# Moving a bias from TensorE to GpSimd in a relational layer, and giving VectorE's small steps two inputs

## The reference

```python
def _layernorm(x, axis=-1, eps=1e-05):
    m = jnp.mean(x, axis=axis, keepdims=True)
    v = jnp.var(x, axis=axis, keepdims=True)
    return (x - m) / jnp.sqrt(v + eps)

def _L0_gnn_ref(x, adj, relation, weight, bias):
    rel_ids = jnp.arange(1, weight.shape[0] + 1, dtype=relation.dtype)
    masks = (relation[None] == rel_ids[:, None, None, None]).astype(x.dtype)
    h = jnp.einsum('rbnm,bmd->rbnd', masks, x)
    y = jnp.einsum('rbnd,rdo->bno', h, weight)
    return y + bias

x = _layernorm(x + _L0_gnn_ref(x, L0_gnn_adj, adj, L0_gnn_weight, L0_gnn_bias), axis=-1)
```

## Time and profile before

| | us |
|---|---|
| median of 3 runs | 119.49 |
| lowest and highest | 118.33, 120.13 |
| the profiled execution | 118.53 |
| its span in the trace | 116.7 |
| busy TensorE, VectorE, ScalarE, GpSimd | 102.6, 95.0, 84.6, 75.7 |

### The profile page before, as it was taken

One profiled execution on the slowest core, in us unless ns is written; L12 is line 12 of the kernel. 1 busy time (PEld: TensorE's weight loads), 2 busy tenths in 40 slices (PEclk: granted clock), 3 DMA queues, 4 the chain that ended last, 5 costly groups with the idle time before them and its releaser, 6 DMA issues.

```text
span 116.7 us, 1943 instructions
## 1 busy us (share of the span) xinstructions
PE 102.6 (88%) x587; PEld 85.5 (73%) x587; DVE 95.0 (81%) x242; ACT 84.6 (72%) x114; POOL 75.7 (65%) x78
## 2 busy tenths in 40 slices
PE   5966379994999999999999999999999999999800
PEld 2333378683889888888898889898888888889600
DVE  0089967633989899999999999999999999996960
ACT  0433199179868997899999999999999889974410
POOL 6069038000095998599759898999899759953640
PEclk9999999999999999999999999999999999999996
DMA  3999999999999999999999999999999997030441
GB/s 87 396 433 429 415 438 427 415 432 418 418 424 424 424 424 417 417 424 424 414 431 421 414 428 413 429 413 427 421 427 418 404 420 314 10 142 38 171 152 53
DMA packets 7362, 42.16 MB, mean 361 GB/s; under 512 B 819, under 2 KB 1206, under 8 KB 3254
## 3 DMA queue, kind: packets, MB, share of 16 engines
q1 hardware_dynamic: 7200, 41.95, 86.9%
q10 hardware_dynamic: 150, 0.07, 0.2%
HBM read 37.82 MB, written 4.19 MB: 360 GB/s over the span
## 4 chain that ended last, share of the span: by engine, by line
PE 48%; DMA 21%; DVE 15%; POOL 8%; issue 3%; ACTq 1%; POOLq 0%; DVEq 0%
PE h_ps L187 32%; DMA adj_sb<-in_adj_dram 17%; PE y_ps L199 8%; PE tp_ps L178 7%; DMA bias_rows<-in_L_gnn_bias_dram 4%; DVE bias_parts L491 4%; POOL scale L217 4%; DVE mask L429 3%; DVE stats L205 3%; POOL x_lo L170 2%; DVE total L443 2%; PE y_ps L194 2%; DVE var_eps L214 2%; DVE mean_var L210 1%; ACTq L379 1%
## 5 line engine op out<-in xcount | busy, mean ns | idle before, releaser
L350 ACT ACTIVATE maskT<-tp_ps 128x2048 fp32r<-128x2048 fp8e5 x32 | 60.2, 1881 | 14.9 <-PE tp_ps L178 14.8
L429 DVE TENSOR_SCALAR mask<-adj_sb 128x2048 uint8<-128x2048 uint32 x32 | 39.5, 1267 | 12.4 <-DMA adj_sb<-in_adj_dram 12.4
L217 POOL TENSOR_TENSOR scale<-var_eps,power 128x4 f32<-128x4 f32 (+1 forms) x17 | 36.3, 2137 | 0.9 <-DVE var_eps L214 0.7
L187 PE MATMUL h_ps<-maskT,x_hi 128*128 128x512 f32 (+1 forms) x144 | 34.2, 379 | 2.6 <-ACT maskT L350 2.5
L187 PE MATMUL h_ps<-maskT,x_lo 128*128 128x512 f32 (+1 forms) x144 | 34.3, 380 | 0.4 <-POOL x_lo L170 0.4
L187 PEld LDWEIGHTS h_ps<-maskT,x_hi 128*128 128x128 f32 x144 | 24.3, 189 | 7.7 <-ACT maskT L350 3.9
L187 PEld LDWEIGHTS h_ps<-maskT,x_lo 128*128 128x128 f32 x144 | 24.1, 189 | 4.5 <-POOL x_lo L170 0.7
L178 PEld LDWEIGHTS tp_ps<-identity,mask 128*128 128x128 f32 x128 | 19.8, 202 | 6.4 <-DVE mask L429 2.7
L178 PE MATMUL tp_ps<-identity,mask 128*128 128x128 f32 x128 | 20.2, 281 | 3.4 <-DVE mask L429 3.4
L170 POOL TENSOR_TENSOR x_lo<-x_sb,x_top 128x1024 fp32r<-128x1024 f32 x8 | 19.2, 2402 | 0.0
L307 POOL TENSOR_SCALAR minus_mean<-mean_var 128x4 f32<-128x4 f32 (+1 forms) x16 | 4.0, 248 | 22.5 <-DVE var_eps L214 21.6
(11 more groups left out here) (30 smaller groups left out, 40.4 us busy)
## 6 DMA issues: line engine op xcount, KB each, us to landing
adj_sb<-in_adj_dram SPq DMA_DIRECT2D x32, 1024.0 KB, 18.0
x_sb<-in_x_dram SPq DMA_DIRECT2D x8, 512.0 KB, 12.1
out_dram<-out_sb SPq DMA_DIRECT2D x7, 512.0 KB, 18.5
out_dram<-out_sb SPq DMA_DIRECT2D x1, 256.0 KB, 2.3
out_dram<-out_sb SPq DMA_DIRECT2D x2, 128.0 KB, 2.6
w_sb<-in_L_gnn_weight_dram ACTq DMA_DIRECT2D x1, 64.0 KB, 7.1
bias_rows<-in_L_gnn_bias_dram ACTq DMA_DIRECT2D x3, 0.5 KB
```

What stands on the lines that cost most here:

```text
L187: last = nc.tensor.matmul(h_ps[:, bank, 0:n], (x_hi, x_lo)[part][:, slot, t, :], maskT[:, places, t // WORD, t % WORD, :], start=(first an ...
L217: nc.gpsimd.tensor_tensor(scale[:, slot, tiles], var_eps[:, slot, tiles], power[:, tiles], ALU.pow).then_inc(done, by)
L350: nc.scalar.activation(maskT[:, u % NMT], turned_codes(u % NTP), ACT.Copy, accum_out=counts[:, u:u + 1]).then_inc(expanded, 1)
L429: nc.vector.tensor_scalar(mask[:, u % NMASK], adj_sb[:, u % NADJ].bitcast(u32), CAP, SET, ALU.min, ALU.mult).then_inc(masked, 1)
```

## The change

The bias no longer goes through TensorE. One transfer spreads it over all partitions, and GpSimd adds it to x in place, once per batch, after the last mask of that batch. VectorE's add waits for that (`biased`). The bf16 parts, their splitting and placing are gone. The variance plus epsilon and the normalising on VectorE take a form with two tensor inputs: epsilon comes from a small tile, and the scale is repeated over 128 columns as the second input. GpSimd takes the scales once for a whole batch, for batches 0 to 5; the last two go in halves and quarters as before. Normalising comes one half later on VectorE and on ScalarE. x_lo of batch 0 is made by VectorE, and GpSimd makes x_lo before x_hi of the following batches. TensorE's projection of half 1 comes one turn earlier.

```diff
-        def spread_bias(y, tiles):
-            n = tiles.stop - tiles.start
-            nc.tensor.matmul(y[:, 0:n, :], spread[:, :], bias_parts[:, 0:n, :], start=True, stop=False)
+        def add_bias(x_slot, done):
+            nc.gpsimd.tensor_tensor(x_sb[:, x_slot], x_sb[:, x_slot],
+                                    bias_rows[:, :].unsqueeze(1).to_broadcast([P, TILES, D]), ALU.add).then_inc(done, 1)
...
-            nc.vector.tensor_scalar(var_eps[:, slot, tiles], mean_var[:, slot, tiles, 1], EPS, None, ALU.add).then_inc(done, by)
+            n = tiles.stop - tiles.start
+            nc.vector.tensor_tensor(var_eps[:, slot, tiles], mean_var[:, slot, tiles, 1], eps[:, 0:n], ALU.add).then_inc(done, by)
...
-                last = nc.vector.tensor_scalar(out_sb[:, b, s, :], total[:, place, s, :], mean_var[:, slot, s, 0:1],
-                                               scale[:, slot, s:s + 1], ALU.subtract, ALU.mult)
+                last = nc.vector.scalar_tensor_tensor(out_sb[:, b, s, :], total[:, place, s, :], mean_var[:, slot, s, 0:1],
+                                                      scale[:, slot, s:s + 1].to_broadcast([P, D]), ALU.subtract, ALU.mult)
...
+            def bias_in(b):
+                if b == 0:
+                    pool.wait_ge(bias_loaded, 16)
+                else:
+                    pool.wait_ge(masked, CH * b + 4)
+                pool.wait_ge(lo_made, b + 1)
+                add_bias(b % NX, biased)
...
             def lo(b):
+                pool.wait_ge(topped, b + 1)
+                if b >= 2:
+                    pool.wait_ge(multiplied, CH * (b - 1))
                 take_lo(nc.gpsimd, b % NX, b % 2, lo_made)
...
-            split_bias()
             hi(0)
-            lo(0)
+            bias_in(0)
             for b in range(B):
                 if b + 1 < B:
+                    lo(b + 1)
                     hi(b + 1)
-                if b >= 1:
+                if 1 <= b < LAST:
+                    scales(b - 1, ALL, CH * b, CH)
+                if b == LAST:
                     scales_half(2 * b - 1)
                 if b + 1 < B:
-                    lo(b + 1)
-                scales_half(2 * b)
+                    bias_in(b + 1)
+                if b >= LAST - 1:
+                    scales_half(2 * b)
...
-            act.wait_ge(bias_cleared, 1)
-            for q in PARTS:
-                act.dma_start(bias_rows[q:q + 1, :], bias.unsqueeze(0)).then_inc(bias_loaded, 16)
+            act.dma_start(bias_rows[:, :], bias.unsqueeze(0).to_broadcast([P, D])).then_inc(bias_loaded, 16)
...
                 expand(2 * hf + 2)
                 expand(2 * hf + 3)
-                if hf >= 3:
-                    finish_half(hf - 3)
+                if hf >= 4:
+                    finish_half(hf - 4)
             copy_half(HALVES - 2)
+            finish_half(HALVES - 5)
             finish_half(HALVES - 4)
...
                 dve.wait_ge(projected, count)
+                dve.wait_ge(biased, b + 1)
...
             convert(0)
             top(0)
-            place_bias()
-            for u in (1, 2, 3):
-                convert(u)
+            dve.wait_ge(topped, 1)
+            take_lo(nc.vector, 0, 0, lo_made)
+            convert(1)
+            convert(2)
+            convert(3)
...
                 add_half(hf - 1)
                 measure_half(hf - 1)
-                if hf >= 2:
-                    finish_half(hf - 2)
+                if hf >= 3:
+                    finish_half(hf - 3)
             find_others()
+            finish_half(HALVES - 4)
             add_half(HALVES - 2)
...
-                spread_bias(y_ps[:, hf % NY], HALF[0])
                 pe.wait_ge(h_copied, 2 * (hf + 1))
...
             pe.wait_ge(weights_loaded, 16)
-            pe.wait_ge(bias_split, 4)
             project_half(0)
```

More of the change, by code:

```diff
@@ L75, in relational_layer @@
         power = sb("power", [P, TILES], fp32)
+        eps = sb("eps", [P, TILES], fp32)
         total = sb("total", [P, NTOTAL, TILES, D], fp32)
@@ L96, in relational_layer @@
         weights_loaded = sem("weights_loaded")
-        bias_cleared = sem("bias_cleared")
         bias_loaded = sem("bias_loaded")
-        bias_split = sem("bias_split")
+        biased = sem("biased")
         const_set = sem("const_set")
@@ L131, in relational_layer @@
         g_split = sem("g_split")
+        g_biased = sem("g_biased")
         g_masked = sem("g_masked")
@@ L151, in flat @@
             return tiles.rearrange("p t d -> p (t d)")
-        def upper(values):
-            return values.bitcast(bf16).rearrange("p (d two) -> p two d", two=2)[:, 1, :]
         def load_adj(eng, b, ch, slot, done):
@@ L198, in project @@
                 for r in range(relations):
-                    last = nc.tensor.matmul(y[:, n, :], h_of(r)[:, s], w_sb[:, r, :], start=False,
-                                            stop=(r == relations - 1 and s == tiles.stop - 1))
+                    last = nc.tensor.matmul(y[:, n, :], h_of(r)[:, s], w_sb[:, r, :], start=(r == 0),
+                                            stop=(r == relations - 1))
             last.then_inc(done, by)
@@ L339, in _ @@
                     nc.gpsimd.tensor_copy(flat(x_hi[:, 0]), flat(x_top[:, :]).bitcast(fp32)).then_inc(g_split, 1)
+                    pool.wait_ge(g_split, 2 * (b + 1))
+                    add_bias(0, g_biased)
                     pool.wait_ge(g_var_ready, b + 1)
@@ L386, in _ @@
             expand(3)
-            for hf in range(1, HALVES - 1):
-                if hf >= 2:
+            expand(4)
+            copy_half(1)
+            expand(5)
+            for hf in range(2, HALVES - 1):
+                if hf > 2:
                     copy_half(hf - 1)
@@ L449, in variances @@
             def variances(b, tiles, count, by):
+                if count == 2:
+                    dve.wait_ge(const_set, 4)
                 dve.wait_ge(measured, count)
@@ L486, in find_others @@
                 nc.vector.tensor_scalar(above[:, 1:2], above[:, 0:1], FULL, None, ALU.is_gt).then_inc(flag_step, 1)
-            def place_bias():
-                dve.wait_ge(bias_split, 3)
-                for q, part in zip(PARTS, (bias_rows, bias_rest, bias_fine)):
-                    last = nc.vector.tensor_copy(bias_parts[q:q + 1], upper(part[q:q + 1, :]).unsqueeze(1).to_broadcast(
-                        [1, HT, D]))
-                last.then_inc(bias_split, 1)
             convert(0)
             top(0)
-            place_bias()
-            for u in (1, 2, 3):
-                convert(u)
+            dve.wait_ge(topped, 1)
[3 more added lines that the diff above has]
+            convert(3)
             top(1)
@@ L541, in _ @@
                     dve.wait_ge(g_projected, 2 * (b + 1))
+                    dve.wait_ge(g_biased, b + 1)
                     for half in range(2):
@@ L626, in _ @@
             turn(5)
+            project_half(1)
             turn(6)
@@ L631, in _ @@
                     turn(2 * hf + 3)
-                project_half(hf - 1)
+                if hf > 2:
+                    project_half(hf - 1)
                 lo_products(hf)
@@ L668, in _ @@
                     for half in range(2):
-                        spread_bias(y_ps[:, half], HALF[0])
                         project(lambda r: h_all[:, r], y_ps[:, half], R, HALF[half], g_projected, 1)
```

18 lines of the change are left out of this document (1 added, 17 removed).

## The result

| | before | after |
|---|---|---|
| median, us | 119.81 | 124.62 |
| lowest and highest | 118.33, 120.80 | 124.55, 125.11 |
| the profiled execution | 118.53 | 124.59 |
| its span | 116.7 | 122.9 |
| busy TensorE, VectorE, ScalarE, GpSimd | 102.6, 95.0, 84.6, 75.7 | 104.6, 98.1, 85.2, 72.7 |

The changed kernel is slower: the ratio is 1.049, with an interval of 1.039 to 1.059. The kernel before spreads from 117.3 to 122.0 us over its runs here and the changed one hardly, and the ratios in this document set a kernel against the faster of those runs, so that they come out up to 2% higher than the ratio of the medians. The forecast was 126.3 us, with a range of 115.5 to 130.

A forecast was written before the change was run, and what follows sets the result against it. TensorE was the nominal bound, with transfer and VectorE right behind. Batch 2 to 3 +1.5, four batches +6.4 and the end -0.5 made +7.4 us on 118.53, 125.9; with the median 1.0 above, 126.3 us, range 115.5 to 130.

The forecast's parts named there:

- F: VectorE's step of two normalised tiles; forecast at 0.65 us instead of 0.51, not held by GpSimd.
- L: VectorE's step of variance plus epsilon; forecast at 0.17 us as before, its hold of up to 1.3 us a batch gone.
- L and F not held: On VectorE beside GpSimd's passes: two SBUF inputs taken as not held, since A (add to total) and S (statistics) are not.
- The order at the end of x_hi: VectorE's next mask, wanted at 2.76 us after T, waits until 3.46; minus_mean and the power stand behind the masks.
- T: VectorE's x_top step, 0.61 us, once a batch; the forecast counts the order from its end.
- rival (a): L and F are held by GpSimd's passes after all; batch 13.9 us, 129.6 us in all; 14 in 100.
- rival (b): The power runs under the masks and costs nothing; batch 11.65 us, 118.6 us in all, no change; 18 in 100.
- Four batches from 3 to 7: Steady part: four batches of 13.15 us instead of 11.56, +6.4 us.
- Batch 2 to 3: From T of batch 2, at 35.11 as before, M M T (two masks, x_top) end at 48.3: 1.5 us later.
- The head: Masks 1 to 3 come some 2 us earlier, but the transfer eats all of it; worth nothing in the sum.
- The end: Behind T of batch 7: three bias matmuls and the stall of L go, one F comes in; -0.5 us.
- Transfer as the bound: A batch brings 4.72 MB, 11.2 us at 422 GB/s; the batch is 11.2 us if VectorE is hardly held.

The follow-up runs named there:

- the run with one row: The changed kernel with the bias transfer to one partition only, the other 127 set to 0 (their output lacks the bias): 123.15 us.
- the kernel where a mask went first: The changed kernel with L as a sum over two columns and F as a reduction over one element that only copies: 125.23 us.

## Why the prediction was right, and where it was wrong

**The time and the sign** were right, 124.6 against 126.3 us, for a reason half right and with luck in the size. Right was that GpSimd's passes hold VectorE more than before: 1.64 us a batch, where the forecast had 0.7 + 1.78 = 2.48. Wrong was where. No mask is held; the largest hold, 0.85 us, is F behind x_hi; the power lies under the masks, and the bias add (56.39 to 58.77) lies in the time without masks after all (55.98 to 59.25) and costs the 0.49 us of L at its end. The bias add out gave a batch of 11.79, as worked out from the trace after. The 126.3 itself stands between the sum's 125.9 and the 126.9 that it gives with the 1.0 us for the median; that choice has no working.

**L and F not held: wrong.** The step reasoned that one SBUF input isn't held and so took two to be free as well. L was held 0.30 and 0.49 us, F 0.85. The Trainium skill, "SBUF — State Buffer", section "Who interferes with whom", gives two SBUF inputs as a ground for contending with a GpSimd instruction that reads SBUF, names tensor_scalar as an operation that can contend through a mode with two ports, and says of tensor_reduce that on this chip it never contends. Which form waits is as the runs show it, though no run here shows the ports: L held as TENSOR_TENSOR (0.46 and 0.65) and as TENSOR_SCALAR (0.46 and 0.65), 0.16 as TENSOR_REDUCE. The forecast looked only at whether the removed form's stall would go, with the row of the held one-input L in the earlier trace rows at hand as a warning against "one input is free".

**The order at the end of x_hi: wrong through the same step.** With L and F free, the mask was to be the one waiting at 3.46 us after T and the power behind it. Because F is held too, F is what waits at the end of x_hi, and minus_mean and the power slip in between its end and the masks. It isn't the hold of L that brings F there: with L in a form that isn't held, the second tile of F still waited for x_hi. So the signs of rival (a) and of rival (b) came up at once, each of which I had priced alone: (a) adds, if elsewhere than it had it (most of it behind x_hi, not behind the bias add), (b) takes away. With both, the batch is 12.28; the forecast said 13.15, (a) 13.9, (b) 11.65. The run with L and F in free forms shows the forecast's own order, with the masks held 0.83 and 1.50 us, and a batch of 12.67.

**Four batches from 3 to 7:** forecast +6.4, measured +3.16, from this.

**Batch 2 to 3:** forecast +1.5, measured +1.68. The size agrees and the mechanism only in part. Up to the scales the order was the forecast's: mask 10 went before x_hi, mask 11 before the power, which then ran alone (1.67 us at 42.15, as estimated from the two shorter ones). The bias add ran from 44.11 to 46.51, 1.0 later than in the sum, which the late head (1.4) accounts for. What it held was L (2.2 us) and not the mask. Without the add the stretch is 11.22 (x_top at 35.94 and 47.16).

**The head: wrong.** "T of batch 2 ends at 35.11 as before", with the one transfer of the bias that "has until that add": the step asked when the bias must be there, not what its 128 rows of 512 bytes take from the other transfers. That was 1.43 us in T of batch 2 and 1.5 in the time, shown by the run with one row (1.47 us less).

**The end:** forecast -0.5, measured +0.07 from the start of T of batch 7 on. The step counted no hold in the first half of batch 7, not even its own 0.7 us; there L and F are held as in every batch, and the masks start 4.46 us behind T instead of 3.37. Of these 1.1 us 0.8 come back as the L of the second half takes 0.65 instead of 1.45, which is the forecast's gain on L in part. The last 0.3 come back in front of the add of half 14: the kernel before stood idle for 0.76 us there, waiting for TensorE's projection (its add starts at 105.98), the changed one had F to do in that place and no wait (112.26). Both adds start 13.6 us behind T, and from there on the two kernels run alike, up to the wait of 0.59 us for the last scale. So the three bias matmuls less gained nothing there: after the change VectorE, not TensorE, is late at that add.

The terms add up to +6.3 us, beside 6.1 between the times of the profiled executions: 1.43 + 1.68 + 3.16 + 0.07. Against the forecast's +7.4 the head is 1.4 more, the order in the steady part 3.2 less, the end and batch 2 to 3 together 0.7 more: two misses of opposite sign leave the sum 1.1 us too high, 1.3 on the profiled execution's time (125.9 against 124.6). That it came so near is luck.

**Transfer as the bound:** the forecast gave the batch 11.2 us when nothing holds VectorE. The version with x_hi on ScalarE and the shift behind the bias add is at 11.21 with the transfer at 420 to 424 GB/s, and none is below. That agrees with the bound, but doesn't show it, as VectorE's own work and holds make 11.18 there.

## What to carry to other kernels

Sort VectorE's small instructions by whether GpSimd's running pass can hold them (in the trace: the same instruction with and without a pass beside it), and draw the order anew with the held ones in front, because the one that waits decides who gets in when the pass ends; freeing one of them alone moves the stall to the next. A long pass of GpSimd belongs beside VectorE's forms that aren't held, and a short dependent step whose result isn't wanted yet belongs behind it. Price a small transfer by what it takes from the others, in the page's GB/s slices, and not by its bytes.

## What the runs showed of the hardware that I had not expected

A transfer that spreads one 512-byte row over 128 partitions, 64 KB in all, lowers the rate from about 430 to about 235 GB/s over a slice of 3.07 us and costs the other transfers 1.6 us; issued later, it costs the same. Why (the row read 128 times, or the many small packets) stays open.

A power for eight columns on GpSimd takes 1.67 us alone, 2.5 under two masks when it starts 0.1 to 0.2 us before them, ending with them, and it ended 1.5 us after them in the kernel where a mask went first. Just ahead of the masks its computing lay under them. Just behind the first one, the bias add that hung on it came 1.0 us later, counted from x_top (8.15 against 7.15), although the masks had been wanted 1.3 us sooner (3.17 against 4.46).

Between two passes of GpSimd one waiting instruction of VectorE got in: L between x_lo and x_hi in the changed kernel (its end at 52.41, x_lo's at 52.38), and one tile of F, not both, with L in the form that isn't held.

The pass with a repeated input (bias_rows over eight tiles) takes 2.38 us like x_lo with two full ones, and F with its scale repeated as a second tensor takes 0.60 for two tiles, like the form with a number per partition: the 0.07 us that the forecast put on it isn't there.
